# TensorE's order within a tick regrouped by tile shape, attend's sums in a PSUM bank of their own

## What is computed

```
# block 0: cross attention on ctx, adaptive norms from cond
q  = ada_ln(x, cond) @ Wq + bq;   k, v = split(ada_ln(ctx, cond) @ Wkv + bkv)
x  = x + softmax(q k^T / sqrt(8)) v @ Wp + bp
# block 1
x  = x + gate_a * (self_attention(modulate(ln(x))) @ W_proj + b_proj)
x  = x + cross_attention(ln(x) @ W_qc, ln(ctx) @ W_kvc) @ W_cproj + b_cproj
x  = x + gate_m * (gelu(modulate(ln(x)) @ W_mlp1 + b_mlp1) @ W_mlp2 + b_mlp2)
```

## Time and profile before

| | |
|---|---|
| median of three runs | 304.66 us |
| the three runs | 302.06, 305.11, 304.66 us |
| profiled execution | 306.48 us |
| its span (first to last instruction) | 304.6 us |
| PE, PE weight loads busy | 264.0 us (87%), 172.7 us (57%) |
| DVE, ACT, POOL busy | 221.8, 221.2, 135.6 us |
| TensorE clock granted, mean | 0.972 |
| DMA | 27.44 MB, mean 90 GB/s |

### The profile page before, as it was taken

One profiled execution on the slowest core, in us unless ns is written; L12 is line 12 of the kernel. 1 busy time (PEld: TensorE's weight loads), 2 busy tenths in 40 slices (PEclk: granted clock), 3 DMA queues, 4 the chain that ended last, 5 costly groups with the idle time before them and its releaser, 6 DMA issues.

```text
span 304.6 us, 10124 instructions
## 1 busy us (share of the span) xinstructions
PE 264.0 (87%) x3811; PEld 172.7 (57%) x3811; DVE 221.8 (73%) x452; ACT 221.2 (73%) x399; POOL 135.6 (45%) x285
## 2 busy tenths in 40 slices
PE   1832869999899998998999999999999999978995
PEld 1521544766556565565666666666656555544875
DVE  6786684997879788797888988889878787322323
ACT  4334277797986969878787787876877879889950
POOL 5350564634436144344574744747338144160500
PEclk9975897999999999999999999999999999999999
DMA  6389342244444454534423343223432200000111
GB/s 192 99 215 271 82 127 61 66 131 110 101 120 101 131 128 101 113 101 110 107 56 79 84 107 107 59 75 88 107 91 73 57 5 3 4 0 2 36 54 52
DMA packets 34223, 27.44 MB, mean 90 GB/s; under 512 B 4904, under 2 KB 33920, under 8 KB 34176
## 3 DMA queue, kind: packets, MB, share of 16 engines
q1 hardware_dynamic: 31750, 24.81, 31.5%
q10 hardware_dynamic: 2426, 2.00, 2.5%
HBM read 6.46 MB, written 1.06 MB: 25 GB/s over the span
## 4 chain that ended last, share of the span: by engine, by line
PE 48%; ACT 15%; DVE 14%; POOL 9%; issue 7%; DMA 3%; ACTq 2%; SPq 1%; POOLq 0%; DVEq 0%
PE all_ps L448 9%; PE all_ps L511 9%; DVE neg_max L920 7%; PE score_ps L474 6%; ACT normed L692 4%; PE keyed_ps L497 4%; PE all_ps L522 4%; PE all_ps L438 3%; PE all_ps L542 3%; PE all_ps L534 3%; POOL rstd L1072 3%; PE all_ps L553 2%; ACT parts L706 2%; POOL parts L1103 2%; DMA stack_k<-parts 2%
## 5 line engine op out<-in xcount | busy, mean ns | idle before, releaser
L920 DVE TENSOR_REDUCE neg_max<-score_ps 128x8 f32<-128x1024 f32 x96 | 116.9, 1218 | 16.7 <-PE score_ps L474 16.3
L726 ACT ACTIVATE probs<-keyed_ps 128x1024 f32<-128x1024 f32 x96 | 98.0, 1021 | 17.8 <-PE keyed_ps L497 17.8
L511 PE MATMUL all_ps<-probs,values 128*32 128x128 f32 x1536 | 61.7, 280 | 0.3 <-ACT probs L726 0.3
L474 PE MATMUL score_ps<-stack_k,stack_q 62*128 62x128 bf16 x768 | 38.6, 220 | 11.7 <-DVE neg_max L920 7.4
L511 PEld LDWEIGHTS all_ps<-probs,values 128*32 128x32 f32 x1536 | 36.5, 109 | 20.0 <-issue 10.4
L474 PEld LDWEIGHTS score_ps<-stack_k,stack_q 62*128 62x128 bf16 x768 | 21.9, 95 | 31.6 <-DVE neg_max L920 18.0
L497 PE MATMUL keyed_ps<-stack_q,stack_k 64*128 64x128 bf16 x768 | 38.1, 219 | 0.9 <-ACT probs L726 0.9
L1088 POOL CAST max_parts<-neg_max 128x16 bf16<-128x16 f32 x48 | 9.7, 202 | 59.3 <-DVE neg_max L920 59.3
L734 ACT ACTIVATE summed<-all_ps 128x256 f32<-128x256 f32 x48 | 18.2, 379 | 18.4 <-PE all_ps L511 18.4
L1072 POOL TENSOR_TENSOR rstd<-var_eps,minus_half 128x4 f32<-128x4 f32 x24 | 24.3, 1016 | 16.0 <-DVE var_eps L885 16.0
L448 PE MATMUL all_ps<-normed_t,w_qk 128*128 128x512 f32 x48 | 30.5, 729 | 0.0
(11 more groups left out here) (103 smaller groups left out, 404.5 us busy)
## 6 DMA issues: line engine op xcount, KB each, us to landing
stack_q<-parts SPq DMA_DIRECT2D x72, 128.0 KB, 2.5
stack_k<-parts SPq DMA_DIRECT2D x66, 128.0 KB, 2.5
gate<-gate_d SPq DMA_DIRECT2D x16, 128.0 KB, 3.4
stack_q<-max_rows SPq DMA_DIRECT2D x96, 4.0 KB
xs<-in_x_dram SPq DMA_DIRECT2D x4, 256.0 KB, 4.2
cs<-in_ctx_dram SPq DMA_DIRECT2D x4, 256.0 KB, 5.0
out_dram<-xs SPq DMA_DIRECT2D x8, 128.0 KB, 1.8
stack_k<-parts ACTq DMA_DIRECT2D x6, 128.0 KB, 4.0
```

Source lines behind the costliest of these rows:

```text
L474: mm = pe.matmul(score_ps[:, e, a * T:(a + 1) * T], stack_q[rows, g % STACKS, CP * c + a, cols], stack_k[rows, g % STACKS, CP * c + a, col ...
L511: mm = pe.matmul(ps[QUAD * a:QUAD * (a + 1), c * T:(c + 1) * T], values[:, u // PER % STACKS, u % PER * PAIRS + CP * c + a, 2 * e:2 * e + ...
L726: act.activation(probs[:, n % 3, :], keyed_ps[:, :, :].rearrange("t e n -> t (e n)"), ACT.Exp, scale=float(D) ** -0.5).then_inc(probs_read ...
L920: dve.tensor_reduce(neg_max[:, u % 2, :, CP * c:CP * (c + 1)], score_ps[:, :, :].rearrange("t e (a k) -> t e a k", k=T), AX.X, ALU.max, ne ...
```

## The change

PE's order in a tick is regrouped, and other queues follow it. Without front work it becomes scores(tick+3, 0), keyed(tick, 0) | attend(tick-1, 1) | turn_attn(tick-2) | scores(tick+3, 1), keyed(tick, 1) | turn_max(tick+2), attend(tick, 0) | turn_summed(tick-1), project_out(tick-2), where a bar is a change of tile shape. turn_attn and attn_with_bias come one tick later, add_branch and add_gated too. The ring of four banks becomes one bank for attend and a ring of three. The front's steps move by a tick, and in ACT's queue both halves of `modulate` (n = 0) stand between the two `exponentials`; in DVE's the statistics, copy_max_rows and divide stand behind the second `row_max`. The loop runs from tick -8 to 57 (before: -6 to 56), and the MLP's ticks are new lists. Ahead of the loop SP waits until the first group's k is in place before it loads further tokens, and the bulk of weights is issued over ticks -8 to -2; POOL clears the second stack before its first roots, DVE the third after the first row_max; ACT's warm-up activation comes before most of its loads.

```diff
-RINGS = (("all", 4),)
+RINGS = (("way_in", 1), ("all", 3))
+RING_KINDS = (("attn",), ("max", "turn", "proj", "out", "cond", "mod", ... "up", "down"))
-        FIRST = -6
-        LAST = 57
-        UP_AT = (40, 42, 43, 44, 44, 44, 45, 47, 48, 48, 48, 49, 52, 52, 52, 52)
-        DOWN_AT = (49, 50, 52, 52, 52, 53, 55, 55)
-        GELU_AT = (48, 49, 52)
+        FIRST = -8
+        LAST = 58
+        UP_AT = (40, 42, 44, 44, 46, 47, 48, 48, 49, 49, 49, 50, 53, 53, 53, 53)
+        DOWN_AT = (48, 50, 51, 52, 53, 55, 55, 56)
+        GELU_AT = (47, 49, 52)
...
             move_parts(0, 0, True)
+            k_in_place(sp, 0)
             load_tokens(2)
-            load_tokens(3)
-            sp.dma_start(wqkv[:, :], L1_xcond_W_qkv).then_inc(loaded["wB"], 16)
...
+            (b_out x3, wp0; then one load_later(i) at the end of each of the ticks -8 to -2)
```

More of the change, by code:

```diff
@@ L44 @@
 AHEAD = 3
-RINGS = (("all", 4),)
-RING_KINDS = (("attn", "max", "turn", "proj", "out", "cond", "mod", "bias", "late", "norm", "q", "k", "v", "gate", "up", "down"),)
+RINGS = (("way_in", 1), ("all", 3))
+RING_KINDS = (("attn",),
+              ("max", "turn", "proj", "out", "cond", "mod", "bias", "late", "norm", "q", "k", "v", "gate", "up", "down"))
 R_Q, R_K, R_V = (0, 3, 6), (1, 4, 7), (2, 5, 8)
@@ L242, in at_tick @@
             uses += [("norm", g, 1)] * (g is not None and g > 1)
-            g = front(tick, -9)
-            uses += [("norm", g, 0)] * (g is not None and g > 1)
+            uses += [("up", n) for n in range(MLP * B // PER) if UP_AT[n] == tick]
+            uses += [("out", tick - 1)] * unit(tick - 1)
+            uses += [("proj", tick - 2)] * unit(tick - 2)
             uses += [("down", n) for n in range(B // 2) if DOWN_AT[n] == tick]
[L246 to L253, removed]
             return uses
@@ L587, in _ @@
                     transpose_normed(g, 1)
-                g = front(tick, -9)
-                if g is not None and g > 1:
-                    transpose_normed(g, 0)
+                for n in range(MLP * B // PER):
+                    if UP_AT[n] == tick:
+                        mlp_up(n // MLP, n % MLP)
+                if unit(tick - 1):
+                    turn_summed(tick - 1)
+                if unit(tick - 2):
+                    project_out(tick - 2)
                 for n in range(B // 2):
@@ L593, in _ @@
                         mlp_down(n // 2, n % 2)
[L594 to L612, removed]
                 if -3 <= tick < 0:
@@ L801, in _ @@
                     clear_values(2)
-                if tick in GELU_AT:
-                    activate_hidden(GELU_AT.index(tick))
+                if unit(tick):
+                    exponentials(tick, 1)
+                g = attention(front(tick, -7))
+                if g is not None:
+                    first_part(g, 1)
+                g = attention(front(tick, -6))
+                if g is not None:
+                    copy_values(g)
+                for n in range(MLP * B // PER):
+                    if UP_AT[n] == tick:
+                        leave_hidden(n)
+                g = front(tick, -8, 1)
+                if g is not None:
+                    modulate(g, 1, True)
                 g = front(tick, -8, 1)
@@ L1003, in _ @@
             fill_stack(1)
-            fill_stack(2)
             row_max(0, 0)
             row_max(0, 1)
+            fill_stack(2)
             for tick in range(FIRST, LAST):
+                if unit(tick + 3) and tick + 3 > 0:
+                    row_max(tick + 3, 0)
+                if unit(tick - 3):
+                    add_branch(tick - 3)
+                g = front(tick, -10, 1)
+                if g is not None and g > 1:
+                    normalise(g, 1)
+                if unit(tick + 3) and tick + 3 > 0:
+                    row_max(tick + 3, 1)
+                g = attention(front(tick, -7))
+                if g is not None:
+                    leave_rest(g, 0)
+                if tick == 3:
+                    late_modulations()
                 g = front(tick, -10)
@@ L1010, in _ @@
                     norm_stats(g, 0)
-                if unit(tick + 3) and tick + 3 > 0:
-                    row_max(tick + 3, 0)
-                if unit(tick - 2):
-                    add_branch(tick - 2)
                 if unit(tick + 2):
                     copy_max_rows(tick + 2)
+                g = front(tick, -12, 1)
+                if g is not None and g > 1:
+                    norm_stats(g, 1)
+                if tick == 1:
+                    copy_gates()
+                if unit(tick - 1):
+                    divide(tick - 1)
                 g = attention(front(tick, -7))
@@ L1036, in _ @@
                         add_mlp(n)
-                g = attention(front(tick, -8))
-                if g is not None:
-                    leave_rest(g, 0)
         @block.gpsimd
```

216 lines of the change are left out of this document (111 added, 105 removed).

## The result

The changed kernel takes 315.25 us (median of four runs, 312.89 to 316.10) beside 304.88 for the kernel before in the same job: ratio 1.0375, 95% interval 1.0312 to 1.0439. It is slower, and outside the predicted range. Its profiled execution took 316.09 us, with a span of 314.3.

A forecast was written before the change was run, and what follows sets the result against it. PE was taken as the bound (94% busy), DVE and ACT close behind, so saved drains were mostly waited for. Middle +1, head -4, late part -1.3 gave -4.3 us: 300.4 us forecast, 289.5 to 308 the range.

The forecast's parts named there:

- rival 1: Whole kernel: the saved tile-change drains reach the end, as ACT's and DVE's queues have slack; 289.5 us, chance 0.2 (whole or half).
- The sum of a second-layer cycle: Four ticks between second scores, second layer's inputs: 4.6+7.1+2.1+5.45 = 19.25 us, where the windows before give 19.15.
- V to N: From the tick with v's products to the tick with ACT's normalise: DVE is late, 4.6 us; PE's savings are lost.
- N to Q: From ACT's normalise tick through turn-and-modulate to the q and k tick: ACT late 7.1 us, then PE 2.1.
- Q to V: From the q and k tick to the v tick: PE is late, 5.25 us and about 0.2 for the bank.
- The waits at the banks: PE with three banks: project_out waits 0.7 for modulate, 0.75 for copy_values, turn_summed 0.2; the first two hidden.
- rival 2: Middle: bank waits not hidden, 0.75 a cycle, 307.2 us (both, 313); sign: project_out's wait in V over 0.6; chance 0.23.
- DVE's normalise of the context: Third layer's inputs, between the two row_max: a 1.0 us row costing 0.4 a cycle, giving about 19.1.
- the first layer's cycle: The one full cycle of first-layer inputs: both loads together and turn_attn waiting for a bank, 0.9 more, 20.1 us.
- the tail: After the last scores: earlier gelus ahead of copy_summed(47), first down filling that hole, last unit a tick more; 0, -3 to +3.
- The head: Ahead of the middle: scores(0) 4 to 5 us earlier through a shorter cast and earlier k; -4 us kept, -1 to -5.5.
- rival 3: Head: its gain is lost in SP's queue, move_max(0) standing behind other issues; 304.4 us, no change, chance 0.15.

The follow-up runs named there:

- norm_tail: Changed kernel with DVE's context normalise a tick later behind the second row_max, and gelus, first down, three ups and adds moved later: 305.72 us, ratio 1.007.
- before_again: The kernel before the change, unchanged, profiled once more: 303.36 us, span 301.5.
- norm_late: Changed kernel with DVE's context normalise back a tick later, behind the second row_max: ratio 1.033 (1.018 to 1.048), span 308.7.
- gelu48: Changed kernel with the first gelus and first down one tick later: 313.0 us, ratio 1.033.
- after: The changed kernel itself, against the kernel before: 315.25 us, ratio 1.0375.
- ring4: Changed kernel with attend back in one ring of four banks and one up moved from tick 44 to 45: 339.54 us, ratio 1.118.
- norm_mod: norm_late with the second half of modulate behind the second exp in ACT's queue, as before the change: 318.25 us, ratio 1.047.
- nt_head0: norm_tail with the head of the kernel before (old load order, second stack cleared behind the roots): 304.75 us, ratio 1.000.
- nt_loads5: norm_tail with the bulk loads issued over ticks -3 to 3 instead of -8 to -2: 304.57 us, ratio 1.005.
- head_only: The kernel before with only the changed kernel's head (load order, POOL's clearing first, loop from -8): 304.45 us, ratio 1.005.

## Why the prediction was wrong

By its parts, in us of span, against the execution that it rests on:

| | forecast | measured |
|---|---|---|
| ahead of tick 4 | -4 | -2.3 |
| ticks 4 to 40 | +1 | +8.2 |
| tick 40 to the end | -1.3 | +3.8 |
| all | -4.3 | +9.7 |

**Right.** A change of tile costs about 0.09: keyed follows scores after 0.23 to 0.24 wherever it doesn't wait, turn_max costs attend 0.01. The drains don't reach the end (against rival 1): with 8.9 us less PE work in 36 ticks (0.25 a tick, forecast 0.32) norm_tail's middle is 1.9 us shorter than before_again's. The sum of a second-layer cycle, 19.25, is right: ticks 12 to 16 and 16 to 20 take 19.02 and 19.45. So are its legs, at full clock: V to N 4.4 to 4.5 (forecast 4.6), N to Q 9.1 to 9.6 (7.1 + 2.1), Q to V 5.43 (5.45). The waits at the banks are 0.73 for copy_values (forecast 0.75), 0.18 in Q (0.2) and 0.29 in T (0.7), and they are covered: in norm_late project_out waits the same 0.73, and V to N takes 4.4. By the prediction's own sign for rival 2, a wait over 0.6 there, the banks would have counted; that sign was wrong.

**The first step that failed: "DVE's normalise of the context (1.0 us between the two row_max) takes 0.4: about 19.1".** It takes 1.3 (V to N 5.73 where norm_late has 4.44). The row was 1.95 us and not 1.0, because the new order puts POOL's work beside it; I had used that very interference to explain the cast of the head, and hadn't asked what POOL does at this place. The place itself was priced rightly: with a row of 1.10 the second row_max would start 0.85 sooner, and 0.45 of the 1.3 would be left (an estimate from these rows, as DVE is the latest in V). V to N comes out at 5.73 to 5.86 against 5.0, 3 us over the four cycles. At full clock such a cycle is 19.7 (gelu48, ticks 32 to 36), not 19.1; norm_late has 18.9.

**The second, and in this execution the larger: the clock, put at nothing.** The sum has no term for TensorE's clock falling in the middle, since the trace of before had it full from 50 us on. Four falls, 17 us at half clock, cost 6.9 us here: 1.1, 1.0 and 2.5 behind the normalise, and 2.3 at tick 9. That last figure holds a wait of 1.04 us ahead of the fall at 87.7 (the program has these scores wait for their q and k in place); the second-layer cycle of ticks 8 to 12, 19.25 in the sum, takes 21.4, and 19.03 in gelu48, which has neither. gelu48 lost 2.3 in its middle. So at full clock the middle of the changed kernel is about 174 us (an estimate: 176.2 less 2.3), and the sum's 173.5 comes close, in part by luck: the normalise takes 3 us more, and the first layer's cycle (ticks 4 to 8), given 20.1, took 19.0. How often the clock falls is in part chance, but not all of it: behind the normalise between the two row_max it fell in three of four places in after, in one of four in gelu48 and in none in ring4; in the five runs with the normalise moved (norm_late, norm_tail, norm_mod, nt_head0, nt_loads5) it fell in none of twenty.

**The third, the tail: "I take 0 for it, bounds -3 and +3", with the gelus ahead of copy_summed(47) and the down in the hole.** +4.5. I had seen the order and priced it at nothing. ACT's rows give the price: 1.64 + 1.28 + 2.19 us between the last attend and its sums, on the path. gelu48 takes 1.3 of it back, norm_tail 2.6; the 1.9 that remain may go with the longer pipe (the last unit's turn_attn and projection come a tick later), which no run separated from the other lists. Ticks 40 to 44 gave back only 0.7.

**The head: "-4 us (bounds -1 and -5.5)".** It gave 2.3 against this base, within the bounds. The cast takes 0.43 us instead of 3.08, and scores(0) start at 23.41, as foreseen. But the base was the late kind of execution (27.72; the other is 24.85, with tick 4 at 60.06, 2.1 us ahead of after's), and rival 3, the queue of SP, took what was left: head_only gains nothing over its own base, nt_loads5 gets 2.5 us back by moving the loads. The prediction gave that rival 0.15.

**Rival 2**, the slower side, had the sign right (0.75 a cycle, 307.2), for a mechanism that ring4 and norm_late show not to be it. The measured time is beyond all the rivals.

Open: the tail's last 1.9 us; what sets off a fall of the clock; and the 0.7 to 2.3 us by which nt_loads5 (37.5 us from its first scores to tick 4) is longer there than the two executions of the kernel before.

## What to carry to other kernels

Before pricing a saved drain, write down for each tick which engine's queue ends last; what PE saves in a tick that DVE or ACT sets is worth nothing, and one microsecond put into that queue can cost more than one, since PE's clock may fall behind the wait. One profile is one execution: before a difference is put down to the change, look where the clock fell in it, and in another execution of the same instructions. When a reordering puts an instruction of DVE beside other work of POOL than before, its duration from the old trace doesn't hold. A ring of buffers goes by the order of uses: regroup the order, and the use that a bank must wait for is another.

## What the runs showed of the hardware

- The clock fell to half after waits none of which was long: in after PE was idle for 0.73, 0.34, 0.28 and 0.80 us between 175.7 and 180.3, and the clock was half from 179.9 for 3.4 us. The same waits of the same instructions stand in gelu48 four times, and it fell behind one of them.
- One execution of norm_late took 382.4 us with a granted clock of 0.568 over the whole span; the other three took 310.5 to 315.1 (its profiled one: 0.949). The cause is not known.
- The same DVE row (tensor_scalar, f32, four of 128x128) took 1.10 us in norm_late, with two short POOL rows (0.24 and 0.22 us) beside it, and 1.95 in after, with POOL's tensor_tensor rows of 1.16, 0.46 and 0.45 us.
